# Scores and attend of a local attention in tiles of 64 rows by 32 columns

## What is computed

```python
def attn_layer(x, Wqkv, qs, ksc, Wo):
    q, k, v = jnp.split(x @ Wqkv, 3, -1)            # x has half its channels shifted by a token
    q, k = l2norm(q) * qs, l2norm(k) * ksc          # per head, 16 heads of 64
    ...                                             # rotary tables with a scale per token
    bk2, bv2 = look(bk), look(bv)                   # the window before and this one: 64 keys
    mask = (it < jb) | (it > jb + w) | (jb == -1)   # w = 32
    sim = jnp.einsum('bhwie,bhwje->bhwij', bq, bk2) * 8.0
    attn = softmax(where(mask, -max, sim))
    out = jnp.einsum('bhwij,bhwje->bhwie', attn, bv2)
    return out.reshape(b, n, 1024) @ Wo
```

## Time and profile before

| | us |
|---|---|
| median of 3 runs | 2099.54 (2096.88 to 2099.59) |
| profiled execution | 2099.2 |
| its span | 2097.7 |
| TensorE busy | 1992.3 |
| ScalarE busy | 1726.7 |
| VectorE busy | 1583.2 |
| GpSimd busy | 1081.7 |

### The profile page before, as it was taken

How to read it: one execution, slowest core, us unless ns; L and a number is a source line. 1 busy time by engine, 2 the same in 40 slices (tenths; PEclk the granted TensorE clock), 3 DMA queues, 4 the chain that set the end, 5 groups by cost and what they waited for, 6 DMA issues and landing times.

```text
span 2097.7 us, 54519 instructions
## 1 busy us (share of the span) xinstructions
PE 1992.3 (95%) x22508; PEld 1635.2 (78%) x22508; DVE 1583.2 (75%) x2244; ACT 1726.7 (82%) x3032; POOL 1081.7 (52%) x529
## 2 busy tenths in 40 slices
PE   5999999679999999999999999999999999999997
PEld 3788888557878788887878787888778787878775
DVE  4555655678888788888888888888888888888874
ACT  2577777558988899988988888989888988989874
POOL 4000000556566765667565766656665657565530
PEclk9899999879999999999999999999999999999998
DMA  5000000023333433243433333333434234433321
GB/s 168 6 10 5 7 7 1 1 80 88 106 84 94 125 92 107 77 119 84 112 97 108 97 106 101 100 99 87 116 88 121 73 90 115 120 91 88 100 77 41
DMA packets 119727, 172.38 MB, mean 82 GB/s; under 512 B 25303, under 2 KB 44346, under 8 KB 119482
## 3 DMA queue, kind: packets, MB, share of 16 engines
q1 hardware_dynamic: 119308, 168.85, 29.6%
q10 hardware_dynamic: 174, 0.05, 0.0%
HBM read 117.48 MB, written 51.38 MB: 80 GB/s over the span
## 4 chain that ended last, share of the span: by engine, by line
PE 74%; ACT 16%; DVE 6%; issue 3%; ACTq 0%; POOL 0%; DMA 0%; DVEq 0%; POOLq 0%
PE o_pair L730 8%; PE bank L660 8%; PE bank L829 7%; PE bank L662 6%; PE bank L661 5%; ACT kT L1044 5%; PE s_pair L703 5%; PE bank L683 4%; PE bank L742 4%; PE bank L715 4%; ACT qT L1036 2%; ACT p L1051 2%; PE s_pair L587 2%; PE bank L587 2%; PE bank L838 1%
## 5 line engine op out<-in xcount | busy, mean ns | idle before, releaser
L1659 POOL TENSOR_TENSOR rt<-raw,rot 128x1024 f32<-128x1024 f32 x192 | 457.4, 2382 | 349.6 <-PE bank L683 242.3
L1668 POOL TENSOR_TENSOR rt<-rt,t 128x2048 f32<-128x2048 f32 x96 | 438.6, 4569 | 179.0 <-DVE t L1459 174.3
L1467 DVE TENSOR_TENSOR rt<-rt,bank 128x2048 f32<-128x2048 f32 x96 | 219.6, 2288 | 107.5 <-POOL rt L1668 105.8
L660 PE MATMUL bank<-wqkv_hi,xs 128*128 128x512 f32 x576 | 271.7, 472 | 8.9 <-ACT vn L1025 3.8
L1008 ACT ACTIVATE raw<-bank 128x512 f32<-128x512 f32 x384 | 229.0, 598 | 60.8 <-PE bank L662 50.0
L1044 ACT ACTIVATE kT<-bank 64x512 f32<-64x512 f32 x384 | 226.9, 591 | 48.5 <-PE bank L683 41.4
L662 PE MATMUL bank<-wqkv_hi,xs 128*128 128x512 f32 x576 | 228.9, 397 | 0.0
L661 PE MATMUL bank<-wqkv_lo,xs 128*128 128x512 f32 x576 | 227.8, 396 | 0.0
L683 PE MATMUL bank<-const,rt 128*128 128x128 f32 x1536 | 215.6, 279 | 12.6 <-DVE zT L1538 6.6
L1459 DVE TENSOR_TENSOR t<-raw,bank 128x1024 f32<-128x1024 f32 x192 | 225.0, 1213 | 0.6
L1446 DVE TENSOR_REDUCE bank<-t 128x32 f32<-128x2048 f32 x96 | 219.2, 2283 | 3.0 <-ACT t L1016 2.9
(11 more groups left out here) (360 smaller groups left out, 4499.7 us busy)
## 6 DMA issues: line engine op xcount, KB each, us to landing
v<-v_rows SPq DMA_DIRECT2D x288, 256.0 KB, 4.5
v_rows<-vn SPq DMA_DIRECT2D x192, 256.0 KB, 3.6
v<-v_rows SPq DMA_DIRECT2D x96, 192.0 KB, 3.2
wraw<-in_L_ffn_Wqkv_dram SPq DMA_DIRECT2D x36, 256.0 KB, 3.0
wo<-in_L_ffn_Wo_dram SPq DMA_DIRECT2D x6, 512.0 KB, 4.1
wraw<-in_L_ffn_W_in_dram SPq DMA_DIRECT2D x8, 256.0 KB, 3.7
w_out<-in_L_ffn_W_out_dram SPq DMA_DIRECT2D x8, 256.0 KB
wraw<-in_L_ffn_W_dram SPq DMA_DIRECT2D x12, 170.5 KB, 3.0
```

The source lines that it names most:

```text
L660: pe.matmul(bank[:, :], hi, w[0][:, :], start=True, stop=False)
L1659: e = pool.tensor_tensor(heads(k.rt_r[c][:, part]), heads(k.raw_r[c][:, part]), cosv, ALU.mult)
L1668: pool.tensor_tensor(k.rt_r[c][:, :], k.rt_r[c][:, :], k.t2[:, :], ALU.add).then_inc(s["rot_add"], 1)
```

## The change

Scores and attend no longer multiply by zero blocks. Each matmul takes one head: 64 rows (the head's own partitions), 32 columns of weights, 64 streamed columns. For each head pair and each window group g there are two matmuls, one for each row half r; row half r writes into bank r of s_pair or o_pair. kT and v2 lose their doubled dimension; kT, pT and oT get two buffers, kT and oT alternating by unit, pT by chunk. The kT evacuation is one instruction of 128 partitions, not two of 64. The mask matmul is split over two row halves of 64, with a spread matrix in place of the identity. VectorE's operations on s_pair and o_pair read by row half. Only the window before the first one is zeroed. The slot tables of all engines, those of the first stages among them, are set anew.

```diff
-    i, j = (np.arange(P) % WIN)[:, None], np.arange(2 * WIN)[None, :]
-    bad = (j < i) | (j > i + WIN)
-    first = bad | ((np.arange(P)[:, None] < WIN) & (j < WIN))
+    k, j = (np.arange(P) % WIN)[:, None], np.arange(2 * WIN)[None, :]
+    below = (np.arange(P) % (2 * WIN) < WIN)[:, None]
+    bad = below & ((j < k) | (j > k + WIN))
+    first = bad | (~below & (j < WIN))
     put("mask", np.stack([np.where(first, f(NEG), f(0)), np.where(bad, f(NEG), f(0))], 1))
+    i = np.arange(P)[None, :]
+    put("spread", np.where(below, i % WIN == k, i == k))
     return out
...
-LATE_START, LATE_SPACING = 392, 32
+LATE_START, LATE_SPACING = 399, 32
...
-PE_AT = dict(qk00=12, qk01=12, qk02=12, qk03=13, qk10=22, qk11=28, qk12=37, qk13=37, v00=44, v01=45, v10=49, v11=50,
-             tqk00=50, tqk01=50, tqk02=56, tqk03=56, tqk10=62, tqk11=62, s00=62, tqk12=67, tqk13=67, s01=67, s10=74,
-             tp00=80, tp01=81, s11=86, a00=86, a01=88, tp10=103, tp11=106, to00=106, to01=106, a10=107, a11=108,
-             to10=115, to11=118, wo=122, mean=136, var=140, up0=151, up1=151, up2=151, down=165)
...
-SP_AT = dict(gain=1, w0=1, w1=4, w2=24, w3=26, st00=26, st01=35, st10=43, st11=43, w4=43, pair0=50, w5=57, pair1=57,
-             wo=117, w6=137, w7=153, w2d=159)
+PE_AT = dict(qk00=5, qk01=8, qk02=9, qk03=10, qk10=17, qk11=26, qk12=28, qk13=29, v00=37, v01=42, v10=44, v11=45,
+             tqk00=45, tqk01=46, tqk02=58, tqk03=58, tqk10=59, tqk11=59, s00=59, tqk12=59, tqk13=59, s01=60, s10=64,
+             tp00=76, tp01=76, s11=80, a00=87, a01=87, tp10=94, tp11=96, to00=97, to01=98, a10=100, a11=101, to10=111,
+             to11=115, wo=123, mean=127, var=132, up0=148, up1=148, up2=148, down=160)
...
+SP_AT = dict(gain=1, w0=22, w1=44, w2=53, w3=53, st00=67, st01=72, st10=74, st11=75, w4=75, pair0=84, w5=84, pair1=84,
+             wo=139, w6=179, w7=198, w2d=198)
...
-QK_EVACS = 6
+QK_EVACS = 4
-KT_ZEROS = 4
-ZEROS = KT_ZEROS + 2 * TC + 2
+KT_ZEROS = 2
+ZEROS = KT_ZEROS + 2
...
         ring = self.ring
         self.qT_r = ring("qT", 2, [P, HP, P])
         self.v_rows = self.nc.dram_tensor("v_rows", (2, S, 2, INNER // 2), F32).ap()
-        self.kT = self.sb("kT", [P, HP, 2, WIN + S])
+        self.kT_r = ring("kT", 2, [P, HP, WIN + S])
         self.vn_r = ring("vn", 2, [P, INNER])
-        self.v2_r = ring("v2", 2, [P, NW, 2, HP * DH])
-        self.oT = self.sb("oT", [P, INNER // P, S])
+        self.v2_r = ring("v2", 2, [P, NW, HP * DH])
+        self.pT_r = ring("pT", 2, [P, HP, P])
+        self.oT_r = ring("oT", 2, [P, INNER // P, S])
     def softmax_buffers(self):
         ring = self.ring
         self.p_r = ring("p", 2, [P, HP, 2, 2 * WIN])
-        self.pT = self.sb("pT", [P, HP, P])
         self.sm_r = ring("sm", 2, [P, 4, HEADS])
         self.oa = self.sb("oa", [P, HP, 2, DH])
...
 def by_head(pair):
-    return pair[:, :].rearrange("p (h j) -> p h j", h=HEADS)
+    return pair[:, :].rearrange("p (r h j) -> p r h j", r=2, h=HP)
+def head_rows(t):
+    return t.rearrange("p (r h) -> p r h", r=2)
...
             v = 2 * u + c
-            bank = one_bank_for(("qkT", 4 * v + n), "qkT", QK_EVACS * v + (n + 1 if n < 2 else 2 * n))
+            bank = one_bank_for(("qkT", 4 * v + n), "qkT", QK_EVACS * v + n + 1)
             if n == 0:
...
                     pe.wait_ge(s["cst"], 1)
-                for n in range(2):
-                    pe.matmul(k.s_pair[:, n * 512:(n + 1) * 512], k.ident_b[:, :],
-                              k.mask_b[:, min(c, 1), :].unsqueeze(1).to_broadcast([P, HP, 2 * WIN]),
+                for r, rows in enumerate(halves):
+                    pe.matmul(k.s_pair[:, r * 512:(r + 1) * 512], k.spread_b[rows, :],
+                              k.mask_b[rows, min(c, 1), :].unsqueeze(1).to_broadcast([DH, HP, 2 * WIN]),
                               start=True, stop=False, skip_group_check=True)
                 pe.wait_ge(s["qkT"], QK_EVACS * (v + 1))
             for hp in range(4 * half, 4 * half + 4):
                 for g in range(NW):
                     k0 = c * P + g * WIN
-                    e = pe.matmul(k.s_pair[WIN * g:WIN * (g + 1), hp * P:(hp + 1) * P],
-                                  qT[:, hp, WIN * g:WIN * (g + 1)], k.kT[:, hp, :, k0:k0 + 2 * WIN],
-                                  start=False, stop=True, skip_group_check=True)
+                    for r, rows in enumerate(halves):
+                        at = r * 512 + hp * 2 * WIN
+                        e = pe.matmul(k.s_pair[WIN * g:WIN * (g + 1), at:at + 2 * WIN],
+                                      qT[rows, hp, WIN * g:WIN * (g + 1)], k.kT_r[u % 2][rows, hp, k0:k0 + 2 * WIN],
+                                      start=False, stop=True, skip_group_check=True)
             if half == 1:
                 e.then_inc(s["pe_s"], 1)
...
                 for g in range(NW):
-                    e = pe.matmul(k.o_pair[WIN * g:WIN * (g + 1), hp * P:(hp + 1) * P],
-                                  k.pT[:, hp, WIN * g:WIN * (g + 1)],
-                                  k.v2_r[c][:, g, :, hp * DH:(hp + 1) * DH], start=True, stop=True)
+                    for r, rows in enumerate(halves):
+                        at = r * 512 + hp * DH
+                        e = pe.matmul(k.o_pair[WIN * g:WIN * (g + 1), at:at + DH],
+                                      k.pT_r[c][rows, hp, WIN * g:WIN * (g + 1)],
+                                      k.v2_r[c][rows, g, hp * DH:(hp + 1) * DH], start=True, stop=True)
             if half == 1:
                 e.then_inc(s["pe_o"], 1)
...
                     act.wait_ge(s["x2"], B)
                 act.activation(k.qT_r[c][:, 4 * n:4 * n + 4, :], src, ACT.Copy).then_inc(s["qkT"], 1)
                 return
-            if n == 2 and c == 0 and u:
-                act.wait_ge(s["pe_s"], 2 * u)
-            if n == 2 and c == 0 and u == 0:
+            if n == 2 and c == 0 and u >= 2:
+                act.wait_ge(s["pe_s"], 2 * u - 2)
+            if n == 2 and c == 0 and u < 2:
                 act.wait_ge(s["zero_kv"], KT_ZEROS)
-            for r in range(2):
-                rows, at = slice(DH * r, DH * (r + 1)), slice(WIN + c * P, WIN + (c + 1) * P)
-                act.activation(k.kT[rows, 4 * (n - 2):4 * (n - 2) + 4, r, at], src[rows], ACT.Copy)\
-                    .then_inc(s["qkT"], 1)
+            act.activation(k.kT_r[u % 2][:, 4 * (n - 2):4 * (n - 2) + 4, WIN + c * P:WIN + (c + 1) * P], src, ACT.Copy)\
+                .then_inc(s["qkT"], 1)
         def exp(c):
             p = k.p_r[c]
         def evacuate_p(c, n):
             v = 2 * u + c
             act.wait_ge(s["pe_pT"], 2 * v + n + 1)
-            if n == 0 and v:
-                act.wait_ge(s["pe_o"], v)
-            act.activation(k.pT[:, 4 * n:4 * n + 4, :], four(k.one.at["pT", 2 * v + n]), ACT.Copy)\
+            if n == 0 and u:
+                act.wait_ge(s["pe_o"], v - 1)
+            act.activation(k.pT_r[c][:, 4 * n:4 * n + 4, :], four(k.one.at["pT", 2 * v + n]), ACT.Copy)\
                 .then_inc(s["pT"], 1)
         def evacuate_o(c, n):
             v = 2 * u + c
             act.wait_ge(s["pe_oT"], 2 * v + n + 1)
-            if c == 0 and n == 0 and u:
-                act.wait_ge(s["pe_wo"], u)
-            act.activation(k.oT[:, 4 * n:4 * n + 4, c * P:(c + 1) * P], four(k.one.at["oT", 2 * v + n]), ACT.Copy)\
+            if c == 0 and n == 0 and u >= 2:
+                act.wait_ge(s["pe_wo"], u - 1)
+            act.activation(k.oT_r[u % 2][:, 4 * n:4 * n + 4, c * P:(c + 1) * P], four(k.one.at["oT", 2 * v + n]), ACT.Copy)\
                 .then_inc(s["oT"], 1)
...
                 dve.wait_ge(s["oa"], v - 1)
                 dve.wait_ge(s["ssum"], v - 1)
-            settle(dve.tensor_reduce(sm[:, 0, :], by_head(k.s_pair), AX.X, ALU.max))
-            dve.tensor_tensor(p[:, :, :, :].rearrange("p h r j -> p (h r) j"), by_head(k.s_pair),
-                              sm[:, 0, :].unsqueeze(2).to_broadcast([P, HEADS, 2 * WIN]), ALU.subtract)\
+            settle(dve.tensor_reduce(head_rows(sm[:, 0, :]), by_head(k.s_pair), AX.X, ALU.max))
+            dve.tensor_tensor(p[:, :, :, :].rearrange("p h r j -> p r h j"), by_head(k.s_pair),
+                              head_rows(sm[:, 0, :]).unsqueeze(3).to_broadcast([P, 2, HP, 2 * WIN]), ALU.subtract)\
                 .then_inc(s["smax"], 1)
         def softmax_sum(c):
             p, sm = k.p_r[c], k.sm_r[c]
             dve.wait_ge(s["exp"], 2 * u + c + 1)
-            settle(dve.tensor_reduce(sm[:, 2, :].rearrange("p (h r) -> p h r", r=2), p[:, :, :, :], AX.X, ALU.add))
+            settle(dve.tensor_reduce(head_rows(sm[:, 2, :]), p[:, :, :, :].rearrange("p h r j -> p r h j"), AX.X, ALU.add))
             dve.reciprocal(sm[:, 3, :], sm[:, 2, :]).then_inc(s["ssum"], 1)
...
             if v:
                 dve.wait_ge(s["pe_oT"], 2 * v)
-            dve.tensor_tensor(k.oa[:, :, :, :].rearrange("p h r e -> p (h r) e"), by_head(k.o_pair),
```

(12 more changed lines are left out.)

60 lines of the change are left out of this document (30 added, 30 removed).

## The result

The changed kernel takes 2037.2 us (median of 4 runs, 2034.3 to 2040.7) against 2098.9 for the kernel before, measured beside it: a ratio of 0.971 with a 95% interval of 0.969 to 0.973. The change brings 62 us; 140 were forecast. Its profiled span is 2034.4 us.

The account below looks back on a forecast made before the run. TensorE, busy 242.84 of 245 us in the middle, was taken as the bound. Small matmuls -154, change of shape -5, idle time +19 make -140 us: from 2099.5 to 1960 us, own range 1925 to 1985; 1925 to 2045 got 0.81.

Parts of the forecast that it names:

- The small matmuls, -154 us: Scores and attend on TensorE: eight tiles stream side by side, each of 384 half blocks falls from 0.87 by 0.40 us.
- the third condition: Scores and attend: whether TensorE can be issued eight matmuls in 0.056 us, one every 7 ns, each with its weight load.
- I take the fast end: Issue pace in small blocks: four starts seen within 30 ns taken as guide to 7 ns, not the sustained 27 ns.
- issue in between: Rival: a matmul with its load takes 10 ns, block 0.64 us, saves 0.20; fetching up to 20 us; 2036 us, chance 0.12.
- Change of shape, -5 us: Mask matmul on TensorE: one more tile shape change per chunk costs 10 to 19 us, its halves side by side save 20.
- ScalarE, 0 us: kT evacuation: 192 of 384 instructions go, 113 us of ScalarE, but beside TensorE's work, so nothing by itself.
- VectorE's strides, second buffers, constants, 0 us: Strided reads by row half, second kT, pT and oT buffers, and the spread matrix's 64 KB load: each taken as nothing.
- Tables, 0 with 8 us either way: New slot tables: first stages reordered, late units 7 slots later; sign not readable from the rows, so 0.
- Idle time of TensorE, +19 us: Per unit, TensorE's idle time grows from 0.3 to 0.7 us as VectorE and ScalarE become 90% busy or more.
- VectorE takes over: Rival: 4.1 us of VectorE's idle time per unit remain, unit 31.9 us; 2009 us, chance 0.17.
- The row halves take turns: Rival: eight tiles need two rounds of 0.056 us, block 0.89 us; 2118 us, chance 0.06.
- issue as the bound: Rival, slower side: each small matmul still takes 27 ns, block 1.74 us, +334 us; 2430 us, chance 0.08.

## Why the prediction was right or wrong

**Where the 62 us come from.** Five kernels form a path, by their ratios to the kernel before: kT in one instruction -0.8% (17 us), the new tables on top of it -0.7% (14 us), scores and mask in small tiles with kT's second buffer -1.9% (41 us), attend in small tiles +0.5% (10 us). The sum is -62. The order of the steps matters: without the first, the tables lose 27 us. The third step has the new mask and kT's second buffer in it, and none of the three was taken apart from the others.

**The small matmuls, -154 us.** The mechanism was right and the term mis-sized. Row halves stream together, starts are 6.7 ns apart, rounds 56 ns, as forecast, but for 32 matmuls only. The failed step is the third condition, "I take the fast end": four starts within 0.03 us are a burst out of a full queue and say nothing on what is sustained. Behind the burst it is 8.35 ns for a matmul and its load at best, 9.75 to 10.3 over a longer stretch. Blocks without their stops fell from 7.80 us a unit (the kernel before in the new order with one kT instruction) to 6.06: 1.74 / 8 = 0.22 us each in place of 0.40, 84 us in all. The stops take back 32, which leaves 52. The rival "issue in between" had this: 10 ns, a block of 0.64, up to 20 us for fetching, 2036 us. Its saving of 0.20 us a block was close to the measured 0.22. That it met the time to 1 us is partly luck: its 2036 leaves its own fetch stops out (up to 20 us, measured 32), and about as much as they cost came back from ScalarE's 17 us and the first stages' 13, which it had left out too. The chance of 0.12 was too small: the trace had nothing between 7 and 27 ns, so it bore no preference for the fast end.

The Trainium skill, TensorE: Matmul & The Clock Gate, Part 1 (architectural detail), gives TensorE a queue of 64 instructions; the break after 32 matmuls with 32 loads agrees with it. Its floor of about 25 ns from start to start doesn't hold between tiles (6.7 ns measured), nor does the 4 ns a tile of its Part 3 hold in fp32 here, neither in the burst nor behind it.

**Change of shape, -5 us.** The mask and its 64 matmuls: 0.525 to 0.319 us from the mask's first start to the scores, against 0.109 to 0.205 us for the last transposition before it, so -0.11 x 96 = -11 us. In size as forecast (-1 to -10). By the records a unit has five groups of small blocks, before and after, not six; as their count stays, the sum doesn't change by it.

**ScalarE, 0 us.** Wrong: 17 us under the old order, 58 under the new. The step read TensorE's busy share and said "beside TensorE's work". But the bank of a transposition is released by the last of the kT evacuations, and the chain passes through four of them in each unit. A busy share of 99% hid it, since a matmul counts as busy for its modelled 0.4 us whether or not the next could have started after 0.23.

**VectorE's strides, second buffers, constants, 0 us.** Right as far as tested: the reduction takes 1225 ns (1222 before) and the product with the reciprocal 1218, as before; pT and oT measured nothing. kT's second buffer was not tried by itself.

**Tables, 0 with 8 us either way.** Wrong in kind. They bring 14 us with one kT instruction and 67 with the whole changed code, and cost 27 in the kernel before. An order can't be priced apart from the work that it orders. The first stages, where code and tables changed together, gave 13 us: the first output projection starts at 490.0 us in place of 502.8 (494.4 with the changed code and the old tables).

**Idle time of TensorE, +19 us.** Forecast 0.7 us a unit, measured 1.5; of these 31.7 / 48 = 0.66 are stops, which the term did not hold, and 0.8 are waits. So apart from the stops its size was right.

**The sum.** Blocks -84, stops +32, mask -11, other waits 0.5 us a unit +25, the hidden wait for kT -17, the first stages -13: -68 us, for -62 measured. The last two overlap in part with the order of the late units, and 6 us stay unexplained.

**The rivals.** "VectorE takes over" has a part: half a microsecond a unit of new waits, 32 us if VectorE had 2.3 us a unit less, but at 84% busy, not at a bound. VectorE itself waits 178.8 us for the scores (7.9 before), where its longest wait was the 105.8 us for GpSimd: the two engines wait for each other in turn. "The row halves take turns" and "issue as the bound" are excluded by the starts in the block.

## What to carry to other kernels

A burst shows what a full queue can do, not what the engine is fed; before tiles are made smaller, ask for a row in which the same count of instructions follows at the same pace for longer than the queue is deep, and if there is none, price the block at both ends and put the forecast between. Smaller tiles paid here in the scores, where half of the blocks stand alone, and not in attend, where they all come in twos, 128 matmuls in a row. Twice the instructions under the old streams already cost a tenth of the block. And follow the whole chain, not its pieces on the busiest engine: an engine that is 99% busy in the profile can still be held once a unit by a neighbour, and the neighbour's saved work then counts.

## What the runs showed of the hardware

- Behind the first 64 instructions, TensorE starts one fp32 matmul of the program text (two loads, two matmuls of 64 columns in the trace) every 16.7 ns at best, 4.2 ns an instruction, and over a long block every 9.75 to 10.3 ns one matmul with its load. This holds for 32 streamed columns as for 64.
- TensorE's instructions come in packets of 16 KB, 256 each, of some 1.1 us. Where blocks ask for them at one instruction in 5 ns, it stops for 0.6 to 3 us: 0.2 us in all with 32 records to a half block, 31.7 with 64, 5.4 with 64 in the scores alone, 193 us with 256 in a pair. With the same instructions in slower blocks it was 17. All 23 gaps of the changed kernel end 1.26 to 1.51 us after a packet's end, which is why I call them fetch stops; what happens in this time no view shows.
- Small tiles of both row halves and four column groups start 6.7 ns apart, and rounds of 64 columns in fp32 follow every 56 ns, for the first 32 matmuls of a block. With 32 columns these 32 start within 162 ns.
- From the last start of a block of 64-column matmuls to the next operation at full width it takes 146 ns, where a stream of 64 columns takes 56.
